# Last stage of a graph-attention and routed-expert kernel: tokens, means and variances are read from PSUM, one power serves two graphs, and stores trail by five graphs

## The reference

```python
moe = jnp.sum(topk_w[..., None] * sel, axis=2)     # the two chosen experts, weighted
y = x + moe                                        # x here: the normalised rows
mu = jnp.mean(y, axis=-1, keepdims=True)
var = jnp.var(y, axis=-1, keepdims=True)
ffn = (y - mu) / jnp.sqrt(var + EPS) * gamma + beta
x = x_before + ffn
```

## Time and profile before

| | us |
|---|---|
| median of 3 runs | 584.8 (584.31 to 587.56) |
| the profiled execution, its own time | 585.1 |
| its span | 583.4 |
| DVE busy in the span | 368.1 (63%) |
| POOL busy in the span | 365.4 (63%) |
| ACT busy in the span | 331.4 (57%) |
| TensorE busy in the span | 439.3 (75%) |

### The profile page before, as it was taken

One profiled execution on the slowest core, in us unless ns is written; L12 is line 12 of the kernel. 1 busy time (PEld: TensorE's weight loads), 2 busy tenths in 40 slices (PEclk: granted clock), 3 DMA queues, 4 the chain that ended last, 5 costly groups with the idle time before them and its releaser, 6 DMA issues.

```text
span 583.4 us, 12194 instructions
## 1 busy us (share of the span) xinstructions
PE 439.3 (75%) x2959; PEld 352.3 (60%) x2981; DVE 368.1 (63%) x1510; ACT 331.4 (57%) x930; POOL 365.4 (63%) x387
## 2 busy tenths in 40 slices
PE   2589999999999999996311797788798889719650
PEld 2257777777777777775310697788687778603210
DVE  1355888888889888778540365555465556507995
ACT  0487777877777777763200465666466666403453
POOL 1101147777777777557772467777777777735886
PEclk9999999999999999999555899999999999958995
DMA  8622333343333443311162567667667667337852
GB/s 253 208 90 92 91 110 123 102 103 101 126 102 125 124 128 105 114 38 38 46 126 71 162 201 222 193 198 217 204 185 223 198 173 228 106 113 243 260 160 90
DMA packets 89156, 84.45 MB, mean 145 GB/s; under 512 B 11192, under 2 KB 75616, under 8 KB 88960
## 3 DMA queue, kind: packets, MB, share of 16 engines
q1 hardware_dynamic: 76560, 62.64, 38.2%
q0 software_dynamic: 8704, 16.93, 8.5%
q10 hardware_dynamic: 3824, 4.11, 2.5%
HBM read 61.39 MB, written 23.28 MB: 145 GB/s over the span
## 4 chain that ended last, share of the span: by engine, by line
DVE 30%; PE 19%; SPq 18%; issue 13%; POOL 8%; DMA 5%; ACT 4%; ACTq 1%; DVEq 1%; POOLq 0%
SPq L364 7%; SPq L362 7%; PE bank L686 4%; DVE prob L891 4%; DVE bn L875 4%; POOL final_rstd L477 4%; SPq L263 3%; POOL expert_bins L428 3%; DVE final_var L1120 3%; DVE no_edge L869 2%; DMA xg<-expert_bins 2%; PE bank L803 2%; DVE x_sb L920 2%; PE bank L810 2%; DVE z L908 2%
## 5 line engine op out<-in xcount | busy, mean ns | idle before, releaser
L469 POOL DMA_INDIRECT expert_results<-y,xg x144 | 143.1, 994 | 62.8 <-issue 32.5
L428 POOL DMA_INDIRECT expert_bins<-row_out,slots x128 | 135.3, 1057 | 42.6 <-issue 30.8
L629 ACT ACTIVATE hidT<-bank,b_cols 128x128 f32<-128x128 f32 x288 | 90.4, 364 | 54.7 <-PE bank L803 47.0
L1086 DVE TENSOR_TENSOR y<-bank,b_all 128x128 f32<-128x128 f32 x144 | 41.9, 291 | 98.8 <-PE bank L810 93.3
L803 PE MATMUL bank<-xgT,w_cur 128*128 128x128 f32 x576 | 89.8, 279 | 9.3 <-ACT xgT L622 5.3
L810 PE MATMUL bank<-w_sb,hidT 128*128 x576 | 89.4, 278 | 1.3 <-ACT hidT L629 1.3
L803 PEld LDWEIGHTS bank<-xgT,w_cur 128*128 128x128 f32 x576 | 77.2, 195 | 10.6 <-ACT xgT L622 6.1
L810 PEld LDWEIGHTS bank<-w_sb,hidT 128*128 128x128 f32 x576 | 75.5, 191 | 1.9 <-issue 1.9
L694 PEld LDWEIGHTS bank<-vh,probT 128*128 128x128 f32 x512 | 64.1, 191 | 20.4 <-issue 13.9
L686 PE MATMUL bank<-featT,qT 128*128 128x512 f32 x128 | 67.1, 606 | 8.9 <-DVE no_edge L869 6.1
L694 PE MATMUL bank<-vh,probT 128*128 128x128 f32 x512 | 68.7, 278 | 3.6 <-DVE probT L899 2.8
(11 more groups left out here) (139 smaller groups left out, 774.0 us busy)
## 6 DMA issues: line engine op xcount, KB each, us to landing
w_cur<-in_L_ffn_w_dram SPq DMA_DIRECT2D x144, 128.0 KB
adj_sb<-in_adj_dram SPq DMA_DIRECT2D x16, 1024.0 KB
xg<-expert_bins SPq DMA_DIRECT2D x144, 65.0 KB
yy<-expert_results SPq DMA_DIRECT2D x16, 512.0 KB, 4.4
x_sb<-in_x_dram SPq DMA_DIRECT2D x16, 256.0 KB
out_dram<-x_sb SPq DMA_DIRECT2D x16, 256.0 KB, 2.3
expert_results<-y,xg POOLq DMA_INDIRECT x144
expert_bins<-row_out,slots POOLq DMA_INDIRECT x128, 3.3
```

The lines of the kernel that those rows point to most:

```text
L428: nc.gpsimd.indirect_dma_start(bins, bass.IndirectOffsetOnAxis(ap=slots[:, r, i, j:j + 1], axis=0), row_out[:, r, j, i, :], None).then_inc ...
L469: nc.gpsimd.indirect_dma_start(results, bass.IndirectOffsetOnAxis(ap=xg[:, t % XS, D:D + 1].bitcast(U32), axis=0), y[:, t % XS, :], None, ...
L629: r = nc.scalar.activation(hidT[:, t % NB, c * P:(c + 1) * P], hidden_of(t, c), ACT.Relu, bias=b1_cols[:, bass.ds(e * FC + c, 1)])
L1086: V.tensor_tensor(y[:, v, :], out_psum(t), b2_all[:, bass.ds(e * D, D)], ALU.add).then_inc(s_biased, 1)
```

## The change

The last stage works in pairs of graphs. `final_mv` moves from SBUF to PSUM bank 3 and gets a third column, set once to the epsilon, so that a tensor_reduce over columns 1 and 2 makes `final_var` (for a tensor_scalar on SBUF before). One `final_power` of 128x8 and one `final_shift` of 128x8 serve two graphs. ACT copies each graph's tokens to PSUM bank g % 3 (`tokens_copy`), one graph ahead of its `normalise`, and DVE's `final_sum` reads them there. On DVE the sums of a pair stand one pair later than the shift; POOL does both gamma products of a pair behind the next pair's power. SP stores five graphs behind.

```diff
-        final_mv = sb("final_mv", [P, VB, TPG, 2])
+        XBB = 3
+        def tokens_psum(g):
+            return bank[g % XBB][:, :].rearrange("p (a d) -> p a d", a=TPG)
+        final_mv = bank[XBB][:, 0:VB * TPG * 3].rearrange("p (v a c) -> p v a c", v=VB, c=3)
...
-                if g >= 3:
-                    sp.wait_ge(s_fo, g - 2)
-                    sp.dma_start(out_v[g - 3], xg_of(g - 3)).then_inc(s_out, 16)
-            for g in range(G - 3, G):
+                if g >= 5:
+                    sp.wait_ge(s_fo, g - 4)
+                    sp.dma_start(out_v[g - 5], xg_of(g - 5)).then_inc(s_out, 16)
+            for g in range(G - 5, G):
...
-            def final_power(g):
-                pool.wait_ge(s_fvar, g + 1)
-                nc.gpsimd.tensor_tensor(final_rstd[:, g % VB, :], final_var[:, g % VB, :], half[:, 0:TPG], ALU.pow).then_inc(s_frs, 1)
+            def final_power(p):
+                v = 2 * p % VB
+                pool.wait_ge(s_fvar, 2 * p + 2)
+                nc.gpsimd.tensor_tensor(final_rstd[:, v:v + 2, :].rearrange("p v a -> p (v a)"),
+                                        final_var[:, v:v + 2, :].rearrange("p v a -> p (v a)"), half[:, :],
+                                        ALU.pow).then_inc(s_frs, 1)
...
-            for g in range(G + 1):
-                if g < G:
-                    final_power(g)
-                if g >= 1:
-                    if g < G:
-                        pool.wait_ge(s_shift, g + 1)
-                    gamma_product(g - 1)
+            for p in range(G // 2 + 1):
+                if p < G // 2:
+                    final_power(p)
+                if p >= 1:
+                    gamma_product(2 * p - 2)
+                    gamma_product(2 * p - 1)
...
+            def tokens_copy(g):
+                act.wait_ge(s_beta, g + 1)
+                wait_for(act, s_fo, g - XBB + 1)
+                nc.scalar.copy(bank[g % XBB][:, :], xg_of(g).rearrange("p a d -> p (a d)")).then_inc(s_xb, 1)
+
+            act.wait_ge(s_biased, XT)
+            tokens_copy(0)
             for g in range(G):
+                if g + 1 < G:
+                    tokens_copy(g + 1)
                 normalise(g)
...
-                    r = V.bn_aggr(final_mv[:, g % VB, i, :], bn[:, i, :])
+                    r = V.bn_aggr(final_mv[:, g % VB, i, 0:2], bn[:, g % 2 * TPG + i, :])
...
-                V.tensor_scalar(final_var[:, g % VB, :], final_mv[:, g % VB, :, 1:2].rearrange("p a b -> p (a b)"), K * K * EPS,
-                                None, ALU.add).then_inc(s_fvar, 1)
+                V.tensor_reduce(final_var[:, g % VB, :], final_mv[:, g % VB, :, 1:3], AX_X, ALU.add).then_inc(s_fvar, 1)
...
-                V.tensor_tensor(xg_of(g), outn[:, g % OB, :, :], xg_of(g), ALU.add).then_inc(s_fo, 1)
+                dve.wait_ge(s_xb, g + 1)
+                V.tensor_tensor(xg_of(g), tokens_psum(g), outn[:, g % OB, :, :], ALU.add).then_inc(s_fo, 1)
...
-            for g in range(G + 3):
-                if g < G:
-                    final_stats(g)
-                if 1 <= g <= G:
-                    final_shift(g - 1)
-                if g < G:
-                    final_variance(g)
-                if 2 <= g < G + 2:
-                    final_sum(g - 2)
+            V.memset(final_mv[:, :, :, 2:3], K * K * EPS).then_inc(s_eps, 1)
+            dve.wait_ge(s_eps, 1)
+            for p in range(G // 2 + 2):
+                if p < G // 2:
+                    final_stats(2 * p)
+                if 1 <= p <= G // 2:
+                    final_shift(p - 1)
+                if p >= 2:
+                    final_sum(2 * p - 4)
+                if p < G // 2:
+                    final_stats(2 * p + 1)
+                if p >= 2:
+                    final_sum(2 * p - 3)
+                if p < G // 2:
+                    final_variance(2 * p)
+                    final_variance(2 * p + 1)
```

More of the change, by code:

```diff
@@ L199, in graph_attention_and_routed_experts @@
         s_sum, s_fs, s_beta = sem("tokens_summed"), sem("final_stats"), sem("beta_added")
-        s_shift = sem("final_shift_made")
+        s_shift, s_xb, s_eps = sem("final_shift_made"), sem("tokens_in_psum"), sem("eps_placed")
         s_fg, s_fmv, s_frs, s_fn, s_fo = sem("gamma_used"), sem("final_var"), sem("final_rstd"), sem("final_normed"), sem("final_made")
@@ L640, in normalise @@
             def normalise(g):
-                act.wait_ge(s_shift, g + 1)
+                act.wait_ge(s_shift, g // 2 + 1)
                 wait_for(act, s_fo, g - OB + 1)
@@ L1104, in final_stats, with final_shift @@
                 for i in range(TPG):
-                    r = V.bn_stats(bn[:, i, :], bank[4 + g % 4][:, i * P:(i + 1) * P])
+                    r = V.bn_stats(bn[:, g % 2 * TPG + i, :], bank[4 + g % 4][:, i * P:(i + 1) * P])
                 r.then_inc(s_fs, 1)
[L1108 to L1111, removed]
+            def final_shift(p):
+                v = 2 * p % VB
+                dve.wait_ge(s_frs, p + 1)
+                V.scalar_tensor_tensor(out=shift[:, v:v + 2, :], in0=final_mv[:, v:v + 2, :, 0:1].rearrange("p v a b -> p v (a b)"),
+                                       scalar=-1.0, in1=final_rstd[:, v:v + 2, :], op0=ALU.mult,
                                        op1=ALU.mult).then_inc(s_shift, 1)
```

## The result

The changed kernel takes 591.5 us (median of 3 runs, 591.34 to 592.85) against 584.8: ratio 1.0105, interval 1.0065 to 1.0145, so slower by about 1%. The forecast was 587.5, with a range up to 590.6. Its profiled execution takes 591.5 us, the span 589.7. The last stage begins with the first load of `yy`, and there the two profiles differ as follows.

What follows compares the result with a forecast made beforehand. The kernel was held bound by a 3.13 us chain per graph, power to final_var, stretched by port blocking. Start 538.51, six pairs of 6.33 and end 5.51 gave 582.00 against 579.30; 584.8 + 2.7 = 587.5 us, range 582.2 to 590.6.

Steps and rivals of the forecast that it cites:

- The ports: Last stage: DVE and POOL shut each other out for 1.35 us a turn, all taken as gone with PSUM operands.
- The power of 128x8: POOL's power for two graphs in the last stage: forecast 1.85 us, its work being paid per column.
- rival (a): POOL's power of 128x8 costs only 1.01 us, so the time is 583.3 us; chance 0.24.
- bn_aggr into PSUM, sums from PSUM, copies: Last stage, DVE and ACT: 0.37 us for four bn_aggr, 0.69 a sum, 0.62 a copy.
- Rival (b): DVE's bn_aggr into PSUM lose their overlap, 0.25 us a graph, giving 591.5 us; chance 0.07.
- w: Length of POOL's power of 128x8 in the last stage, taken as 1.85 us.
- loop 1: Last stage, power, gamma product, two sums and variances: 4.48 + w a pair, 6.33 us forecast.
- loop 2: Last stage, from sum through copies, normalises, TensorE, statistics, variances, power and gamma: 10.69 + w for two pairs, 6.27 us a pair.
- The start: Start of the last stage: the first sum at 538.51 us, 4.9 late, since both graphs' statistics come first.
- TensorE at full clock: Last stage: the forecast's 6.33 us a pair assumes TensorE's clock does not fall despite 2.6 us idle per pair.
- rival (c): TensorE's clock falls to 1.2 GHz in the last stage: 7.0 to 7.1 us a pair, 592 us; chance 0.05.
- The sum: Whole last stage: the last final_sum starts at 582.00 us against 579.30, 2.7 later, giving 587.5 us.

Runs made afterwards that it cites:

- e1: Kernel before without POOL's wait for the next shift ahead of each gamma product, all operands still in SBUF; 587.72 us, ratio 1.0035.
- d3: Kernel before with only means and variances in PSUM and the reduce for final_var, tokens in SBUF, wait for the shift kept; ratio 0.9952.
- e2: Kernel before with means and variances in PSUM, the reduce, and the wait for the shift dropped; tokens stay in SBUF; 573.15 us, ratio 0.9777.
- c3: Changed kernel with ScalarE's two lines swapped, so tokens_copy of the next graph stands behind normalise; 585.24 us, ratio 1.0013.
- c2: c1 with two more 128x512 products on TensorE after each pair but the last, read by nobody; 587.45 us, ratio 1.0050.
- e4: Changed kernel itself, timed again on the same chip as others; 590.88 us, ratio 1.0089.
- d2: c4 with POOL's wait for the next shift ahead of each gamma product put back; ratio 0.9967.
- c4: Kernel before, graph by graph in its old order, with the changed one's PSUM operands, copies and reduce, and no wait for the shift; 573.10 us, ratio 0.9782.
- c1: Changed kernel with final_mv (three columns) in SBUF instead of PSUM; 590.18 us, ratio 1.0093.
- d1: Changed kernel with both variances of a pair ahead of the two sums on VectorE, and token copies behind both normalises; ratio 0.9888.

## Why the prediction was wrong, step by step

- **The ports: right.** 1.35 us of mutual blocking a turn was there and is gone: final_var 0.17, sum 0.68, no stretched power. The Trainium skill, page "SBUF — State Buffer", section "Who interferes with whom", says that a VectorE instruction with two SBUF inputs contends with a GpSimd instruction that reads SBUF, and that the order of issue decides who blocks. The traces agree where a shift starts behind a gamma product (e1: 1.22 in place of 0.16) and where a power starts behind a sum (1.49 in the earlier trace rows, 1.38 in e1); they do not where a sum starts behind a power: 0.07 us behind in d3 and 0.04 in e2, and the power takes 1.01 and the sum 0.69 or 0.70, neither stretched.
- **The power of 128x8: right in kind, the size a little off.** 1.64 us, not 1.85 and not the 1.01 of rival (a). Four more columns cost 0.63. If every column costs the same, which two lengths cannot show, that is 0.16 a column and 0.38 paid once. Over six pairs the shorter power gave back 1.0 us of the forecast.
- **bn_aggr into PSUM, sums from PSUM, copies: right.** 162 ns against 156 each and 0.37 to 0.38 for four; 682 against 692; copies 0.60 for 0.62. Rival (b) is out, and the Trainium skill's higher fixed cost of a VectorE instruction that reads PSUM ("VectorE: DVE Perf Modes", section "The TRN2 errata — SBUF-src ops pay a fixed extra latency per instruction") doesn't show in these rows.
- **The loops: right in form.** With w = 1.64 loop 1 gives 6.12 a pair (c3: 6.04) and loop 2 gives 12.33 for two (c2: 12.30). Loop 2 holds TensorE's rows once in two pairs, so with 5.37 in place of 3.87 it gives 13.83; measured 13.81.
- **The start: right in kind, too large.** Forecast 4.9 us late, measured 3.4 from the first load. The shorter power gives back 0.2 for each of two; the rest is luck: TensorE's clock rose earlier in this execution, and the second graph's statistics started 9.8 us after the first load, 10.8 in the kernel before. In the fourteen profiles this time lies anywhere from 9.4 to 11.0, in changed and unchanged orders.
- **The step that failed is TensorE at full clock.** I wrote rival (c), priced it at 7.0 to 7.1 us a pair and 592 us, and gave it 0.05, because the clock had taken 2.6 us of idleness to fall at the end of the kernel before and the new gaps were to be 2.6. The new gaps of 1.9 to 2.7 come again and again, and the clock fell in every second pair: 6.9 us a pair in place of 6.33. Six pairs at 6.9 in place of the 6.17 that loop 2 gives at full clock are 4.4 us. c2 shows that it is the cause; the repetition e4 has the same turn of 3.87 and 5.37 us.
- **The sum.** The last sum starts at 585.7, forecast 582.0. Of the 3.7 us, 3.5 arise between the first and the last sum (47.0 against 43.5, about the clock's 4.4 less the power's 1.0), 1.7 lie ahead of the stage and are scatter, and the start gave 1.5 back. The time lies 0.9 us above the range, less than that scatter; it took the clock and some of the scatter to get there (e4: 590.9). Without the clock's 4.4 us the time would have been near the forecast, by an estimate from these numbers, but partly because misses of either sign cancel.
- **What I did not see at all:** the wait for the shift, which the changed kernel drops as well (`s_shift` in the diff). I gave its removal no price. In the kernel before it is worth nothing alone (e1), and with the mean in PSUM 0.7 us a graph (d2 against c4), the better part of the gain that was to be had.

Where did the ports' gain go? Into the order. Unpaired, and with the wait dropped, it is 12 us (e2). Paired, it is lost: the power stands ahead of the gamma products on POOL, the sums that need them stand ahead of the variances on DVE, and the next power needs those: a serial loop of 6.1 us a pair. The copies tied normalise, and by it TensorE, to the same sums; that gave TensorE its long gaps, and with the fallen clock a pair takes another 0.7 us. The late first sum costs 3.4 us on top. c4 and e2 beat both kernels; e2 is the simpler one.

## What to carry to other kernels

Freeing an engine pays only if what it waits for isn't queued behind the freed work: write the loop over one period through all queues, waits for buffers too, before pairing or batching. Ask of a wait that looks useless what it keeps apart, and when an operand moves, ask again. Where TensorE is fed in bursts with gaps of some 2 us, price its work at half clock as well.

## What the runs showed of the hardware

- The granted clock of TensorE stood at 0.50 in every second pair of the changed kernel, first after gaps of 2.19 and 2.15 us with 3.87 us of work between them; c1 and e4 repeat it. In d1 it fell after a single gap of 2.20 us behind 10.11 us of work, while in the changed kernel the gap of 2.19 behind 9.07 us of work left it at 1.00. In c3, with gaps of 0.37 and 1.76 us in a pair, it stayed at 1.00.
- DMA moved 362 to 371 GB/s in the full windows of 5 us in c4; the last stage before had 271 in the turn of the earlier trace rows, and 247 to 318 in such windows from 535 to 560.
- POOL's power took 1.01 us on four columns and 1.64 on eight, where a product of 512 columns took 1.26.
- Two instructions on DVE and POOL that both read SBUF stretched the later one to 1.22 us (shift behind gamma, e1), 1.49 and 1.38 (power behind sum); a sum that started 0.04 to 0.07 us behind a power was not stretched, nor was the power (d3, e2). With the mean in PSUM the shift took 0.14 (e2).
